# Differential attention, 128 quads of heads: the sums leave the accumulator by ScalarE as columns, are multiplied by GpSimd, and are transposed once per quad

## The reference, cut to what matters

```python
scores = jnp.einsum('bhqd,bhkd->bhqk', q, k)                 # 32 score heads of 8, per batch
probs = jax.nn.softmax(scores.astype(jnp.float32), axis=-1)
lam = (lam1 - lam2 + LAMBDA_INIT)
probs = probs.reshape(b, H, 2, s, s)
w = probs[:, :, 0] - lam * probs[:, :, 1]
attn = jnp.einsum('bhqk,bhkd->bhqd', w, v)                   # v: 16 columns per head
rms = jax.lax.rsqrt(jnp.mean(attn * attn, axis=-1, keepdims=True) + EPS)
attn = attn * rms * subln_g
```

## Time and profile before

| | |
|---|---|
| time, median of 3 runs | 6063.33 us (6057.4 to 6066.57) |
| profiled execution | 6064.04 us, span 6062.2 us |
| busy share of the span | TensorE 93%, VectorE 91%, ScalarE 80%, GpSimd 33% |
| mean granted TensorE clock | 0.970 of full speed |
| 1000 to 5000 us, all inside `attend` | VectorE 99%, TensorE 98% busy, 3339 maxima |

### The profile page before, as it was taken

How to read it: one execution, slowest core, us unless ns; L and a number is a source line. 1 busy time by engine, 2 the same in 40 slices (tenths; PEclk the granted TensorE clock), 3 DMA queues, 4 the chain that set the end, 5 groups by cost and what they waited for, 6 DMA issues and landing times. The chain is left out here.

```text
span 6062.2 us, 166095 instructions
## 1 busy us (share of the span) xinstructions
PE 5630.7 (93%) x50896; PEld 2015.1 (33%) x50896; DVE 5537.9 (91%) x6200; ACT 4845.1 (80%) x8950; POOL 2006.0 (33%) x3781
## 2 busy tenths in 40 slices
PE   8878999999999999999999999999999999987775
PEld 4542233333333333333333333333233323325424
DVE  7868999999999999999999999999999999967706
ACT  5755888888888888889888888888888888873304
POOL 7981222222222222222222222222222222225406
PEclk9997999999999999999999999999999999998877
DMA  5672222222232222222222222222222222216598
GB/s 178 203 202 49 49 52 52 51 52 52 52 52 51 52 51 52 51 50 52 52 47 51 52 51 48 51 51 51 50 52 52 52 52 51 52 35 199 173 359 272
DMA packets 436840, 493.13 MB, mean 81 GB/s; under 512 B 99283, under 2 KB 298099, under 8 KB 436195
## 3 DMA queue, kind: packets, MB, share of 16 engines
q1 hardware_dynamic: 435171, 483.57, 32.7%
q10 hardware_dynamic: 1024, 0.53, 0.0%
HBM read 360.60 MB, written 123.21 MB: 80 GB/s over the span
## 5 line engine op out<-in xcount | busy, mean ns | idle before, releaser
L677 ACT ACTIVATE at_e<-at_ps_e 128x512 f32<-128x512 f32 x8192 | 4368.8, 595 | 542.5 <-PE at_ps_e L766 373.2
L691 DVE TENSOR_REDUCE at_largest<-at_ps_m 128x1 f32<-128x1024 f32 x4096 | 4671.1, 1202 | 56.2 <-PE at_ps_m L795 53.0
L782 PE MATMUL at_ps_o<-at_e,at_v 128*32 128x256 f32 (+1 forms) x30720 | 2687.1, 422 | 12.3 <-issue 8.2
L795 PE MATMUL at_ps_m<-k_stack,q_stack 48*128 48x512 bf16 x8192 | 2500.1, 385 | 132.7 <-DVE at_largest L691 58.3
L766 PE MATMUL at_ps_e<-q_stack,k_stack 51*128 51x512 bf16 x8192 | 2505.7, 383 | 5.2 <-issue 2.3
L782 PEld LDWEIGHTS at_ps_o<-at_e,at_v 128*32 128x32 f32 x30720 | 845.0, 149 | 1567.3 <-issue 935.0
L766 PEld LDWEIGHTS at_ps_e<-q_stack,k_stack 51*128 51x128 bf16 x8192 | 598.1, 93 | 1678.3 <-ACT at_e L677 1641.0
L596 POOL TENSOR_TENSOR at_negated<-at_zeros,at_largest_t 128x32 f32<-128x32 f32 x256 | 64.7, 253 | 3262.7 <-DVE at_largest_t L698 3262.7
L795 PEld LDWEIGHTS at_ps_m<-k_stack,q_stack 48*128 48x128 bf16 x8192 | 607.6, 93 | 203.5 <-DVE at_largest L691 172.2
L639 POOL TENSOR_TENSOR at_rms<-at_mean_eps,at_minus_half 128x16 f32<-128x16 f32 x128 | 372.7, 2912 | 10.0
L436 PE MATMUL pr_ps_q<-pr_xn_t,pr_w 128*128 128x512 f32 x512 | 232.3, 596 | 2.0 <-issue 1.3
(11 more groups left out here) (130 smaller groups left out, 2856.0 us busy)
## 6 DMA issues: line engine op xcount, KB each, us to landing
k_stack<-k_parts SPq DMA_DIRECT2D x1536, 64.0 KB
q_stack<-q_parts SPq DMA_DIRECT2D x256, 192.0 KB
q_stack<-q_parts SPq DMA_DIRECT2D x256, 128.0 KB
w_first<-in_w SPq DMA_DIRECT2D x32, 1024.0 KB, 11.7
ex_w_second<-in_w SPq DMA_DIRECT2D x32, 1024.0 KB, 12.7
q_parts<-pr_parts SPq DMA_DIRECT2D x96, 256.0 KB, 2.4
k_parts<-pr_parts SPq DMA_DIRECT2D x96, 256.0 KB, 2.8
pr_x_in<-in_x SPq DMA_DIRECT2D x16, 1024.0 KB, 5.8
```

The costliest lines, as they stand in the source:

```text
L677: nc.scalar.activation(e[:, j % E_BUFS], ps_e[:, bank(u, j)], ACT.Exp, scale=SCALE).then_inc(exp_done, 1)
L691: nc.vector.reduce_max(largest[:, u % 2, j // SIDE, j % SIDE:j % SIDE + 1], ps_m[:, j % 2], AX.X).then_inc(max_done, 1)
L782: last = nc.tensor.matmul(ps_o[32 * tile:32 * tile + 32, columns], v[:, u, tile // 2, kt::TILES], e[:, (QUAD * g + tile) % E_BUFS, columns ...
L795: last = nc.tensor.matmul(ps_m[:, j % 2, half * HALF:(half + 1) * HALF], q_stack[rows, u, pair, c, t * P:(t + 1) * P], k_stack[rows, u, pa ...
```

## The change

- `v` gets a block of ones in front of the values too. For c = 0 the stationary operand is values then ones, for c = 1 ones then values. So `ps_o` holds U1 over s1 for c = 0 and s2 over U2 for c = 1, row under row, and a plain product of the two gives U1 s2 in 16 rows and U2 s1 in the 16 others.
- ScalarE copies `ps_o` to `sums` (`copy_sums`) after 7 of the 32 exponentials that follow a softmax's last; it frees `ps_o` now, and VectorE's two `turn_sums` of 512 columns are gone.
- s1 and s2 themselves are needed for the epsilon: SyncE moves one row of each, reshaped, by eight small transfers per quad (`move_totals`, 2 KB each, SBUF to SBUF). The four for c = 0 are issued after `load_v`, the four for c = 1 between `load_stacks` and `store`.
- GpSimd multiplies 512 and then 32 columns into `crossed`; VectorE transposes its 544 columns once per quad, at g = 5 of the next quad. GpSimd's `finish` has 14 operations instead of 15. `turn_out` moves from g = 7 to g = 11.
- Where loops are cut on VectorE and ScalarE, and the numbers `ACT_HEAD`, `DVE_HEAD` for the loops' start, follow from this.

```diff
-        PE_HEAD, ACT_HEAD, DVE_HEAD = 200, 160, 176
+        PE_HEAD, ACT_HEAD, DVE_HEAD = 200, 144, 192
...
+            DVE_HEAD_PERIODS, TURN_SUMS, TURN_OUT = 12, 5, 11
+            COPY_AT = QUAD * LAG - 1
+            TOTAL_DMAS = 2 * QUAD
...
+                def move_totals(n, c):
+                    sp.wait_ge(sums_read, 2 * n + c + 1 + 1)
+                    sp.wait_ge(crossed_done, 2 * n + 2)
+                    for g in range(QUAD):
+                        row = 32 * g + (0 if c else VD)
+                        sp.dma_start(totals[32 * g:32 * g + BLOCKS, c], sums[row:row + 1, c]).then_inc(totals_moved, 16)
...
                         load_rows(n + AHEAD, (u + AHEAD) % BUFS, 0)
                         load_v(n + AHEAD, (u + AHEAD) % BUFS)
+                    move_totals(n, 0)
+                    if rows:
                         load_rows(n + AHEAD, (u + AHEAD) % BUFS, 1)
                     if load:
                         sp.wait_ge(scores_done, HALVES * (n + 1))
                         load_stacks(n + BUFS, u)
+                    move_totals(n, 1)
                     store(n, u)
...
+                    if not (isinstance(n, int) and n == 0):
+                        pool.wait_ge(sums_turned, n)
+                    nc.gpsimd.tensor_tensor(crossed[:, 0:HALF], sums[:, 0], sums[:, 1], ALU.mult).then_inc(crossed_done, 1)
+                    pool.wait_ge(totals_moved, 16 * TOTAL_DMAS * (n + 1))
+                    nc.gpsimd.tensor_tensor(crossed[:, HALF:], totals[:, 0], totals[:, 1], ALU.mult).then_inc(crossed_done, 1)
+                    pool.wait_ge(sums_turned, n + 1)
+                    by_block = crossed_t[:, 0:HALF].rearrange("p (b v) -> p b v", v=2 * VD)
+                    s1_s2 = crossed_t[:, HALF:HALF + BLOCKS]
+                    nc.gpsimd.tensor_tensor(second[:], by_block[:, :, VD:],
+                                            neg_lam[:].unsqueeze(2).to_broadcast([P, BLOCKS, VD]), ALU.mult).then_inc(pool_step, 1)
+                    nc.gpsimd.tensor_tensor(both[:], s1_s2, s1_s2, ALU.mult).then_inc(pool_step, 1)
                     pool.wait_ge(pool_step, base + 1)
-                    nc.gpsimd.tensor_tensor(normed[:, 1], sums_t[:, 1, :, 0:VD],
-                                            scaled_s1[:].unsqueeze(2).to_broadcast([P, BLOCKS, VD]),
-                                            ALU.mult).then_inc(pool_step, 1)
+                    nc.gpsimd.tensor_tensor(attn[:], by_block[:, :, 0:VD], second[:], ALU.add).then_inc(pool_step, 1)
...
+                def exponentials(n, u, first, end):
+                    for j in range(first, end):
+                        act.wait_ge(scores_done, HALVES * n + j + 1)
+                        if j % QUAD == 0:
+                            act.wait_ge(sums_done, GROUPS * n + j // QUAD + 1 - E_GROUPS + E_GROUPS)
+                        nc.scalar.activation(e[:, j % E_BUFS], ps_e[:, bank(u, j)], ACT.Exp,
+                                             scale=SCALE).then_inc(exp_done, 1)
+                def copy_sums(n, c):
+                    act.wait_ge(sums_done, GROUPS * n + TILES * (c + 1) + E_GROUPS)
+                    act.wait_ge(crossed_done, 2 * n + 2)
+                    nc.scalar.copy(sums[:, c], ps_o[:]).then_inc(sums_read, 1)
+                def turn(n, u, last):
+                    exponentials(n, u, COPY_AT, HALVES // 2 + COPY_AT)
+                    copy_sums(n, 0)
+                    exponentials(n, u, HALVES // 2 + COPY_AT, HALVES)
+                    if not last:
+                        exponentials(n + 1, (u + 1) % BUFS, 0, COPY_AT)
+                    copy_sums(n, 1)
...
-                def turn_sums(n, c):
-                    dve.wait_ge(sums_done, GROUPS * n + TILES * (c + 1) + E_GROUPS)
-                    nc.vector.transpose(sums_t[:, c].rearrange("p b d -> p (b d)"), ps_o[:]).then_inc(sums_read, 1)
+                def turn_sums(n):
+                    dve.wait_ge(crossed_done, 2 * (n + 1) + 2)
+                    nc.vector.transpose(crossed_t[:], crossed[:]).then_inc(sums_turned, 1)
...
-                    if g == LAG - 1 and last_quad:
-                        turn_sums(n - 1, 1)
-                    if g == HEAD - 1 and last_quad:
+                    if g == TURN_SUMS and last_quad:
+                        turn_sums(n - 1)
+                    if g == TURN_OUT and last_quad:
                         turn_out(n - 1, u - 1)
-                    if g == TILES + LAG - 1 and this_quad:
-                        turn_sums(n, 0)
...
+                    first = (0 if c else VD * TILES) + kt
                     for tile in range(QUAD):
                         last = nc.tensor.matmul(
-                            ps_o[32 * tile:32 * tile + 32, columns], v[:, u, tile // 2, kt::TILES],
+                            ps_o[32 * tile:32 * tile + 32, columns],
+                            v[:, u, tile // 2, first:first + 2 * VD * TILES - kt:TILES],
```

More of the change, by code:

```diff
@@ L492, in attend @@
             parts = sb("parts", [P, PARTS, BLK], BF16)
-            sums_t = sb("sums_t", [P, 2, BLOCKS, BLK])
-            scaled_s1, both = sb("scaled_s1", [P, BLOCKS]), sb("both", [P, BLOCKS])
-            normed, attn_t = sb("normed", [P, 2, BLOCKS, VD]), sb("attn_t", [P, BLOCKS // 2, 2, VD])
+            sums, totals = sb("sums", [P, 2, HALF]), sb("totals", [P, 2, BLK])
+            crossed, crossed_t = sb("crossed", [P, HALF + BLK]), sb("crossed_t", [P, HALF + BLK])
+            second, both = sb("second", [P, BLOCKS, VD]), sb("both", [P, BLOCKS])
+            attn_t = sb("attn_t", [P, BLOCKS // 2, 2, VD])
             attn, square = sb("attn", [P, BLOCKS, VD]), sb("square", [P, BLOCKS, VD])
@@ L586, in _ @@
             def _(pool):
-                nc.gpsimd.memset(v[:, :, :, VD * TILES:], 1.0).then_inc(ones_set, 1)
+                nc.gpsimd.memset(v[:, :, :, 0:VD * TILES], 1.0).then_inc(ones_set, 1)
+                nc.gpsimd.memset(v[:, :, :, 2 * VD * TILES:], 1.0).then_inc(ones_set, 1)
+                nc.gpsimd.memset(totals[:], 1.0).then_inc(ones_set, 1)
+                pool.sem_inc(crossed_done, 2)
                 nc.gpsimd.memset(zeros[:], 0.0).then_inc(ones_set, 1)
@@ L628, in finish @@
                     nc.gpsimd.tensor_tensor(square[:], attn[:], attn[:], ALU.mult).then_inc(pool_step, 1)
-                    step = 8
+                    step = 5
                     width = VD // 2
@@ L669, in _ @@
                 act.sem_inc(exp_done, SLOTS)
-                with hinted(nc, act, 0, loops + 1, slot=ACT_HEAD) as i:
-                    for u in range(BUFS):
-                        n = BUFS * i + u
-                        for j in range(HALVES):
-                            act.wait_ge(scores_done, HALVES * n + j + 1)
-                            if j % QUAD == 0:
-                                act.wait_ge(sums_done, GROUPS * n + j // QUAD + 1 - E_GROUPS + E_GROUPS)
-                            nc.scalar.activation(e[:, j % E_BUFS], ps_e[:, bank(u, j)], ACT.Exp,
-                                                 scale=SCALE).then_inc(exp_done, 1)
+                act.sem_inc(sums_read, 1)
+                def exponentials(n, u, first, end):
[16 more added lines that the diff above has]
+                    copy_sums(n, 1)
+                exponentials(0, 0, 0, COPY_AT)
+                with hinted(nc, act, 0, loops, slot=ACT_HEAD) as i:
+                    for u in range(BUFS):
+                        turn(BUFS * i + u, u, False)
+                for u in range(BUFS):
+                    turn(BUFS * loops + u, u, u == BUFS - 1)
             @block.vector
@@ L739, in _ @@
                                         ALU.add).then_inc(lam_done, 1)
-                for g in range(HEAD):
+                for g in range(DVE_HEAD_PERIODS):
                     period(0, 0, g, True, rows=False, last_quad=False)
                 def turn(n, u, tries, next_tries, rows):
-                    for g in range(HEAD, GROUPS):
+                    for g in range(DVE_HEAD_PERIODS, GROUPS):
                         period(n, u, g, tries, rows)
-                    for g in range(HEAD):
+                    for g in range(DVE_HEAD_PERIODS):
                         period(n + 1, u + 1, g, next_tries, rows)
```

24 lines of the change are left out of this document (7 added, 17 removed).

## The result

The kernel with the change takes 7913.19 us (median of 4 runs, 7902.51 to 7930.03), the kernel before beside it 6061.75 (4 runs, 6057.4 to 6066.57): ratio 1.3057, interval 1.303 to 1.3083, 1851 us slower. The forecast was 7545 us with a range of 7130 to 7880. Its sign and its main mechanism hold; its size falls short by 368 us, and the time lies 33 us above the range.

A forecast was written before the change was run, and what follows sets the result against it. VectorE was taken to bound the kernel, with practically no idle time in a quad of 37.9 us. +11.9 us per quad for 124 quads: 6064 + 1476 + 5 = 7545 us, range 7130 to 7880.

The forecast's parts named there:

- The queue's order and the landing with the stacks: SyncE: totals issue behind stacks (ending 13.0 to 14.2 us after quad origin O), landing with them, O + 21.5.
- The wait of 10.5 us: VectorE at the transposition, g = 5: waits from O + 11.4 to O + 21.9 for GpSimd's product, 10.5 us.
- What the wait sets off: TensorE halts during VectorE's wait and its clock is halved afterwards: 1.7 us per quad, 1.5 to 3.
- The output's store: SyncE: next c = 0 maxima queue behind the later output; about even, 0 to 1 us; 0.3 with ScalarE's copy.
- -0.59: VectorE: two 512-column transpositions go and one of 544 comes, saving 0.59 us per quad, 76 us if nothing else happened.
- Sum: Per quad: -0.59 + 10.5 + 1.7 + 0.3 = +11.9 us, for 124 quads 1476 us.
- slower still: Quad: stacks end at O + 24, or clock costs 3 us and maxima's load 1: 7850 to 8050 us; chance 0.06.
- The rival of the other sign: Faster: totals' product ready by O + 12.0, VectorE's wait hidden; 0.59 us per quad gained, 5988 us; chance 0.03.

The follow-up runs named there:

- part 3: The changed kernel with each quad's output stored behind the next c = 0 maxima instead of in front of them; 7814.74 us (1.2899).
- part 4: The changed kernel with both moves: c = 1 totals in front of the stacks, next c = 0 maxima in front of the output; 6074.23 us (1.0022).
- the version with the totals first: The changed kernel with the four c = 1 totals transfers issued in front of the 18 stack loads; 6280.96 us (1.0355).
- the 6011 us version: part 4 with stacks issued behind the values, and c = 1 totals ahead of the c = 1 maxima; the fastest, 6011.31 us (0.9909).
- the stacks' new place: The kernel before with its stacks issued in the quad's second half, behind the values; 6027.52 us (0.9931).
- the filler: The changed kernel with ten additional float32 matmuls of 512 columns per quad at g = 6, results not read; 7820.29 us (1.2887).

## Why the prediction was right, and where it was not

- **The queue's order and the landing with the stacks: right.** Issue of the stacks ends at O + 13.3 on average (O + 13.0 to 14.2 forecast); the totals land with the stacks' data, whatever queue issues them. The wait stands at the transposition, in every quad.
- **The wait of 10.5 us:** measured 11.2 (11.3 in the stretch above). The stacks' data land at O + 22.3 on average (I took 21.5) and the transposition starts 1.1 us behind that (I took 0.4). VectorE arrives at O + 12.2 and not 11.4, which hides part of it: with the late output undone (part 3) it arrives at O + 11.6, and the wait is 12.2.
- **"What the wait sets off", 1.7 us:** right in kind, and inside the stated 1.5 to 3. Three of four quads lose 2.24 us, 0.5 more than I took; the quads behind a loop's turn lose less than before, since the long wait hides their own halt, and in the mean 1.46 is left. My row was a halt of 4.6 us, and the length of the halt turned out not to matter between 5 and 11 us.
- **"The output's store ... it is about even: 0 to 1 ... I take 0.3" is the step that failed.** The 0.3 was for the copy too, in which part 4 found no loss. The late output costs 1.3 us per quad by itself (158 us in the kernel before), 207 us in the version with the totals first, and 98 in the changed kernel, where the great wait absorbs part. My working set the chain of 8.5 to 9 us against nine steps, 10.2, less what TensorE is ahead, found them even, and then charged near nothing; the trace has TensorE waiting for `max_parts` up to 2.7 us, and the maxima behind it for attempts. Against the version with both moves, the changed kernel comes 0.64 us later to its transposition and needs 16.58 instead of 15.22 us for the last 13 steps of the quad: 2.0 us together. 1.8 of them go when the store is moved (part 3), for 1.0 more of the wait. With this step undone the kernel takes 7814.74 us, inside the range.
- **"-0.59" for VectorE's transpositions:** the instruction cost what I said (0.745 us), but only 0.3 us per ordinary quad comes out (37.91 to 37.63). The ten maxima in front of the transposition now come every 1.146 us ((11.52 - 1.21)/9 in the row below, of the 6011 us version) and not every 1.13, and one step of 1.25 us stands at O + 22; elsewhere the step is still 1.13. The first part of the prediction says that a saving counts until TensorE's own pace is reached, and the sum left that out; that it is this pace is argued, no run isolates it. The quads behind a turn lose 1.4 us each by the fetches, so that the mean quad gains nothing (+0.1).

```profile
3021.49 11.52 DVE L735 TENSOR_REDUCE at_largest<-at_ps_m 128x1 f32<-128x1024 f32 x10
```

- **Sum:** +0.1 + 11.2 + 1.46 + 2.0 = +14.8 us per quad instead of +11.9, times 124 = 1835, and 1851 were measured. The excess of 2.9 is 0.7 from each of the wait and the lost saving, 1.7 from the late output, less 0.2 for the clock (0.5 more in three of four quads, set against the halts that the wait hides in the fourth).
- **The rivals:** "slower still" (7850 to 8050) holds the time, but neither of its conditions is met as it stands: the stacks land at O + 22.3 and not 24, and the clock costs 2.24 us and not 3. The late output's 2.0 brings the time there, with a little from every other term. I gave it 0.06 because I let the small terms vary together only a little. The rival of the other sign, a saving in full (76 us), shows nowhere: the fastest version is 51 us below the kernel before, of which the stacks' new place alone gives 43, and the change adds some 16 us to them, which the two intervals do not tell from nothing.

Open: why the packets of instructions are late in some turns and not in others is not settled (before, every fourth turn is late, the 1st, 5th, 9th and so on, most of the others hardly), nor what takes the remaining 1 us in every quad behind a turn.

## What to carry to other kernels

When a small transfer is on the way of a result, ask what bytes are still moving on the DMA engines when it is issued, and not only what stands ahead of it in its queue: here four transfers of 2 KB cost 11 us per quad behind 1,536 KB (when they go first there is no wait, and all eight transfers of a quad cost 54 us in the whole kernel), and another issuing engine did not help. Each time that an operation moves, go through the whole queue once more for what now stands behind it (output, maxima, values, totals and instruction fetches took turns as the late one here), and price it by the consumer's slack in steps, with nothing rounded to even. An instruction taken from the bounding engine gains only until the next engine's pace, which must stand in the sum.

## What the runs showed of the hardware

- Small transfers issued behind bulk loads complete with them: the totals' last count came 0.68 to 0.82 us behind that of the stacks in each of 110 quads of the changed kernel. Issued from ScalarE's queue they landed 7.6 us on average after their issue, behind the loads of SyncE's queue; issued ahead of the stacks, in the version with both moves, they land 1.1 us after it.
- Packets of instructions come late behind bulk loads: up to 3.5 us and more in the kernel before, with TensorE idle up to 5.4 us as a result (8.1 in the version with both moves). With the loads issued in the other half of the quad that idle time was at most 1.0 us, in the kernel before as in the change.
- A halt of TensorE of 5 or of 11 us costs some 2.2 us more than its length, lost with the clock at 0.50 after it: where the filler kept the clock full, the steps behind the wait took 9.43 us, otherwise 11.35.
